# Four PSUM banks as one pool for turns, small products and down results

## The chip, the cores and the metric

The kernel runs on one core of one Trainium2 chip. The metric is the device time of one execution in microseconds; the kernel before takes 510.87 us, the median of three runs (510.63 to 511.22).

## What is computed

Eight sequences of 512 tokens of 128 features pass through three blocks: a mixture of experts with half weight, a linear attention with rotary positions, a short convolution and an output gate, and the same mixture of experts once more.

```python
x = L0_attn_hidden_states                       # (8, 512, 128), fp32
x = x + 0.5 * _L0_ffn_ref(_layernorm(x), ...)   # "layer 1"
x = x + _L0_attn_ref(_layernorm(x), ...)        # "layer 2"
x = x + 0.5 * _L0_ffn_ref(_layernorm(x), ...)   # "layer 3", same weights as layer 1

# _L0_ffn_ref: one shared expert, and the best 2 of 8 routed experts, each 128 -> 256 -> 128
shared = (silu(x @ shared_gate.T) * (x @ shared_up.T)) @ shared_down.T
probs = sigmoid(x @ router_w.T + routing_bias)
scores, indices = top_k(probs, 2); scores = scores / sum(scores)
g, u = silu(x @ gate_w[e]), x @ up_w[e]
out = shared + sum over the two chosen e of score_e * ((g * u) @ down_w[e])

# _L0_attn_ref: q, k, v, gate projections; 8 heads of 16
num = q @ (k.T @ v) * scale + sum(v);  den = q @ sum(k) * scale + seq_len
out = ((num / den + depthwise_conv5(v)) * (x @ Wg.T)) @ Wo.T
```

## The kernel before, in words

The work is cut by batch b (0 to 7; 512 tokens are 4 tiles of 128) and by layer (1, 2, 3). Batches form groups (`GROUPS`: three in layer 1, four in layer 3), and a group is routed as a whole. Its tokens are sorted by expert into rows in DRAM, 128 to a block: GpSimd scatters normalized tokens (L1151), SyncE loads blocks two at a time as a *pair* r (92 pairs, `xb`), and results go back by a store (L736) and by GpSimd's gathers (L1172). VectorE adds them to X (L1238).

A pair passes through these steps, each with an engine and a line:

- `pair_turn` (TensorE, L822): transposes of `xb` into the PSUM bank `xt_ps`; `pair_hi` (ScalarE, L1014) and `pair_lo` (VectorE, L1201) read it, as an fp32 number is multiplied as a high and a low part.
- `front` (TensorE, L839 to L841): gate and up product of one block, three matmuls of 512 columns. A unit has two halves, one bank each; its first is named j = 1. Two such units of two banks, `gu0` and `gu1`, are taken in turn. Shared experts (units S) and attention projections (units A) pass through them too (L799 to L801).
- `silu` (ScalarE, L1025) and `hid` (VectorE, L1215; L1219 for the shared expert), which makes `hs`.
- `hidden_turn` (TensorE, L872): transposes of `hs` into the bank `ht_ps`; `hT_copy` (ScalarE, L1031) copies it.
- `down` (TensorE, L881): the down product, into the first bank of the pair's own gate/up unit; `y_copy` (ScalarE, L1006) copies it out and so frees the bank. `store` follows.

PSUM has eight banks of 128 x 512 fp32: four for `gu`, one each for `ht_ps` (hidden turns, and shared down products, L892, read by L1228) and `xt_ps`, and two, `misc0` and `misc1`, for all small products: turns of normalized tokens (L908), logits (L922, L924), counts (L937), and in attention k-v products, denominators, their spreading, numerators and the output projection (L947 to L981). VectorE gives back most of them: L1271, L1284, L1367, L1456, L1461, L1471, L1486. Before the change a logits result of one group can be read into `L` only when the group before has its probabilities.

The order on each engine is written out by a planner (class `Plan`). It knows each operation's length in units of 10 ns (a front half is 73, a copy of 512 columns 50), and draws 600 random sets of shifts of the ranks; for each it schedules greedily, on the engine that is free first the ready operation of least rank among those that can start within `NEAR` = 10 units, and keeps the shortest plan. Engines then run in order, held by semaphores. `take` makes TensorE wait for the last reader of a bank before it writes there. GpSimd's scatters and gathers are spaced 160 units by the plan, except those of the first group.

```python
PACE, HOP, NEAR = 160, 16, 10
...
def take(bank, done, value):
    if bank in held:
        once.wait_ge(*held[bank])
    held[bank] = (done, value)
```

Of the kernel before, what the change touches and what calls it, by code (L numbers as in the profile page):

```python
# [6 lines left out]
P = 128  # L7
# [9 lines left out]
T = S // P  # L17
# [18 lines left out]
XT, XB, HB, YB, GB, YG, ROOMS = 6, 5, 4, 3, 3, 3, 2  # L36
# [37 lines left out]
class Plan:  # L74
# [96 lines left out]
    def route(self, i, l, g):  # L171
# [40 lines left out]
    def routed(self, r, l, g, n):  # L212
# [9 lines left out]
        op(("pair_turn", r), "PE", 25, ("load", r), back("pair_lo", 1), ("squares",))  # L222
# [5 lines left out]
        op(("hidden_turn", r), "PE", 45, ("hid", u), back("hidden_turn", 1))  # L228
# [5 lines left out]
    def attention(self, b):  # L234
# [37 lines left out]
    HELD = {"turn": "lo", "logits": "bias", "count": "based", "kv": "mask", "den": "invert", "spread": "rden_bc", "num": "attend", "project": "attended"}  # L272
# [77 lines left out]
    def schedule(self, rank):  # L350
# [4 lines left out]
        self.misc, self.xt_of, self.yg_of = {}, {}, {}  # L355
        bank = [None, None]
        ht = [None]
# [38 lines left out]
        def dynamic(key):  # L396
# [24 lines left out]
            if name in ("hidden_turn", "sdown"):  # L421
                return after(ht[0]) if ht[0] else 0
# [14 lines left out]
        def settle(key, t):  # L437
# [7 lines left out]
            if name == "hidden_turn":  # L445
                ht[0] = ("hT_copy", key[1])
            if name == "sdown":
                ht[0] = ("add", key[1], key[2], "shared")
                self.shared_order.append(key[1:3])
            if name in self.HELD:  # L450
                i = min((i for i in range(2) if not bank[i] or after(bank[i]) is not None),
                        key=lambda i: after(bank[i]) if bank[i] else 0)
                self.misc[key], bank[i] = i, (self.HELD[name], *key[1:])
            if name == "hi":
                i = min((i for i in range(XT) if not xt[i] or after(xt[i]) is not None),
# [63 lines left out]
def build(nc, x, wq, wqp, wk, wv, wg, wo, lepe_w, lepe_b, sgate, sup, sdown, gate_w, up_w, down_w,  # L519
# [8 lines left out]
    with ExitStack() as ctx:  # L528
# [10 lines left out]
        ht_ps = ps("ht_ps")  # L539
        xt_ps = ps("xt_ps")  # L540
        m0, m1 = ps("misc0"), ps("misc1")
# [40 lines left out]
        L, neg, pos = [sb(name, [P, TMAX, E]) for name in ("L", "neg", "pos")]  # L582
# [122 lines left out]
        def misc(*key):  # L705
            return (m0, m1)[plan.misc[key]]
# [80 lines left out]
        def _(pe):  # L787
# [30 lines left out]
            def pair_turn(r):  # L818
                once.wait_ge(xb_loaded[r % XB], 16 * (r // XB + 1))
                wait(once, xbt_lo_done, r)  # L820
                for j in range(width(*plan.pair[r])):
                    mm = pe.transpose(xt_ps[:, j * P:(j + 1) * P], xb[r % XB][:, j], ident)  # L822
# [44 lines left out]
            def hidden_turn(r):  # L867
                n = nth_hidden["R", r]
                once.wait_ge(h_done, n + 1)
                take("ht", hT_done, r + 1)  # L870
                for q in range(HALVES * width(*plan.pair[r])):
                    mm = pe.transpose(ht_ps[:, q * P:(q + 1) * P], hs[n % HB][:, q * P:(q + 1) * P], ident)  # L872
# [13 lines left out]
            def shared_down(l, b):  # L886
                once.wait_ge(h_done, nth_hidden["S", l, b, 1] + 1)
                take("ht", updated[b], update(l, b, "shared"))
                for t in range(T):
                    for half in range(HALVES):  # L890
                        m = nth_hidden["S", l, b, half]
                        mm = pe.matmul(ht_ps[:, t * D:(t + 1) * D], hs[m % HB][:, t * P:(t + 1) * P],  # L892
# [3 lines left out]
            def multiply_ones(n):  # L896

                for _ in range(n):
                    pe.matmul(xt_ps[:].rearrange("p (t n) -> p t n", t=T), ones_bf[:],
                              ones_bf[:].rearrange("p (o n) -> p o n", o=1).to_broadcast([P, T, P]), start=True, stop=True)  # L900

            def xn_turn(l, b):
# [4 lines left out]
                for t in range(T):  # L907
                    mm = pe.transpose((m0, m1)[m][:, t * P:(t + 1) * P], xn[:, b, t], ident)  # L908
                mm.then_inc(xnT_ready[l], 1)
                if (l, b) == (1, 0):  # L910
                    multiply_ones(WARM // 2)

            def logits(l, b):
# [4 lines left out]
                dst = (m0, m1)[m]  # L918
# [8 lines left out]
            def count(l, g):  # L927
# [5 lines left out]
                dst, n, c = (m0, m1)[m], tiles(l, g), chosen[l, g]  # L933
# [7 lines left out]
            def kv(b):  # L941
# [4 lines left out]
                for t in range(T):  # L946
                    mm = pe.matmul((m0, m1)[m][:, 0:VW], k_rot[:, t, :], v_tok[:, t, :], start=t == 0, stop=t == T - 1)  # L947
                mm.then_inc(kv_ready, 1)

            def denominators(b):  # L950
# [4 lines left out]
                for t in range(T):  # L955
                    mm = pe.matmul((m0, m1)[m][:, t * NH:(t + 1) * NH], q_rot[:, t * P:(t + 1) * P], ks_bd[:],
# [3 lines left out]
            def spread(b):  # L960
# [4 lines left out]
                for t in range(T):  # L965
                    mm = pe.transpose((m0, m1)[m][:, t * P:(t + 1) * P], wide[:, t * P:(t + 1) * P], ident)
                mm.then_inc(rbc_ready, 1)

            def numerators(b):
# [4 lines left out]
                pe.matmul((m0, m1)[m][:], kv_bd[:], q_rot, start=True, stop=True).then_inc(num_ready, 1)  # L974

            def out_project(b):
# [3 lines left out]
                for t in range(T):  # L980
                    mm = pe.matmul((m0, m1)[m][:, t * D:(t + 1) * D], oT[:, t * P:(t + 1) * P], wo_sb[:],  # L981
# [4 lines left out]
            multiply_ones(WARM)  # L986
# [6 lines left out]
        def _(act):  # L993
# [8 lines left out]
            def y_copy(r):  # L1002
# [3 lines left out]
                nc.scalar.activation(ys[r % YB][:].rearrange("p j d -> p (j d)")[:, 0:n], bank(("R", r))[:, 0, 0:n],  # L1006
                                     ACT.Copy).then_inc(y_copied, 1)

            def pair_hi(r):
# [4 lines left out]
                nc.scalar.activation(xbt_hi[r % 2][:, 0:n], xt_ps[:, 0:n], ACT.Copy).then_inc(xbt_hi_done, 1)  # L1014
# [12 lines left out]
            def hT_copy(r):  # L1027
# [3 lines left out]
                nc.scalar.activation(hT[r % 2][:, 0:n], ht_ps[:, 0:n], ACT.Copy).then_inc(hT_done, 1)  # L1031
# [155 lines left out]
        def _(dve):  # L1187
# [8 lines left out]
            def pair_lo(r):  # L1196
# [4 lines left out]
                v.tensor_tensor(xbt_lo[r % 2][:, 0:n], xt_ps[:, 0:n], xbt_hi[r % 2][:, 0:n].bitcast(F32),  # L1201
# [359 lines left out]
```

## Time and profile before

| what | value |
|---|---|
| median of three timed runs | 510.87 us |
| profiled execution, span | 540.9 us, 30.0 us above that median |
| TensorE matmul busy | 474.9 us (88%) |
| TensorE weight load busy | 381.7 us (71%) |
| VectorE busy | 348.5 us (64%) |
| ScalarE busy | 272.3 us (50%) |
| GpSimd busy | 282.4 us (52%) |

The profile is of one execution, on the only core. A busy share is the part of the span in which the engine ran an instruction; the table by stretch gives the same for parts of the span. "Idle before" is the time an engine stood before an instruction, and the releaser is whose semaphore ended it; "issue" is standing for which the profile has no reason. Matmul ends are modelled, so TensorE's busy time covers some of its standing. Timelines give start and length in microseconds.

### The profile page before, as it was taken

The page shows a single profiled execution, that of the slowest core. Times are in us where ns is not written, and L with a number is a line of the kernel's source. Part 1 is how long each engine was busy: PE and PEld are TensorE (multiplying, and loading weights), DVE is VectorE, ACT ScalarE, POOL GpSimd, SP SyncE. Part 2 cuts the span into 40 slices and gives each one's busy share as a digit, 9 for nine tenths or more (in the row PEclk, how much of TensorE's full clock was granted, in tenths as well). Part 3 has the DMA queues.
Part 4 walks back from the last instruction along what each step waited for, and adds up shares of the span by engine and source line. Part 5 has one row for each costly group of instructions (what it writes and reads, how often), then busy time and mean ns, then how long its engine had stood idle before and what let it go on. Part 6 is the DMA issues. An engine that isn't in the chain of part 4 may idle for free.

```text
span 540.9 us, 9674 instructions
## 1 busy us (share of the span) xinstructions
PE 474.9 (88%) x2975; PEld 381.7 (71%) x2975; DVE 348.5 (64%) x1064; ACT 272.3 (50%) x612; POOL 282.4 (52%) x290
## 2 busy tenths in 40 slices
PE   7894687998999999999999999999999998899980
PEld 3673676776777787777877777877777776667760
DVE  4992795322358765889996789998966224344442
ACT  5861232555566466647647556653554543443530
POOL 4167054545566506666715666776555545553543
PEclk9999799999999999999999999999999999999997
DMA  8961112234431223321132321113442433442222
GB/s 240 377 215 55 54 64 68 79 112 130 121 89 55 87 80 109 103 65 58 57 102 75 86 66 59 45 45 93 121 133 82 127 95 92 124 127 59 79 73 68
DMA packets 74352, 53.66 MB, mean 99 GB/s; under 512 B 9664, under 2 KB 68928, under 8 KB 74304
## 3 DMA queue, kind: packets, MB, share of 16 engines
q1 hardware_dynamic: 66112, 36.26, 22.4%
q0 software_dynamic: 8192, 16.79, 10.0%
q8 instruction: 26, 0.43, 0.3%
q14 instruction: 22, 0.18, 0.1%
HBM read 26.87 MB, written 26.15 MB: 98 GB/s over the span
## 4 chain that ended last, share of the span: by engine, by line
PE 53%; DVE 23%; issue 8%; ACT 7%; another core or an unknown queue 4%; DMA 2%; POOL 1%; SPq 1%; DVEq 0%; POOLq 0%; ACTq 0%
PE gu L881 15%; PE ht_ps L872 7%; PE gu L839 6%; PE gu L841 6%; PE gu L840 5%; PE xt_ps L822 3%; DVE hs L1219 2%; DVE hs L1215 2%; ACT gs L1025 2%; PE gu L799 2%; DVE raw L1415 2%; PE gu L801 1%; PE gu L800 1%; ACT xn L1048 1%
## 5 line engine op out<-in xcount | busy, mean ns | idle before, releaser
L1172 POOL DMA_INDIRECT yg<-y_sorted,places x128 | 123.0, 961 | 113.2 <-PE gu L841 72.4
L1151 POOL DMA_INDIRECT x_sorted<-xn,places x128 | 129.9, 1015 | 97.3 <-PE gu L841 36.2
L881 PEld LDWEIGHTS gu<-w,hT 128*128 128x128 f32 x708 | 87.1, 191 | 36.0 <-issue 33.7
L881 PE MATMUL gu<-w,hT 128*128 x708 | 100.3, 284 | 11.3 <-ACT hT L1031 6.7
L1025 ACT ACTIVATE gs<-gu 128x512 f32<-128x512 f32 x124 | 72.2, 583 | 53.5 <-PE gu L801 19.4
L1215 DVE TENSOR_TENSOR hs<-gs,gu 128x512 f32<-128x512 f32 x92 | 60.7, 662 | 49.6 <-ACT gs L1025 27.0
L839 PE MATMUL gu<-w,xbt_hi 128*128 x177 | 83.6, 473 | 7.1 <-ACT ys L1006 2.9
L1031 ACT ACTIVATE hT<-ht_ps 128x512 f32<-128x512 f32 x92 | 53.3, 580 | 56.6 <-PE ht_ps L872 38.8
L1201 DVE TENSOR_TENSOR xbt_lo<-xt_ps,xbt_hi 128x256 fp32r<-128x256 f32 x92 | 37.7, 410 | 64.9 <-ACT xbt_hi L1014 56.5
L841 PE MATMUL gu<-w,xbt_hi 128*128 x177 | 70.7, 399 | 0.0
L840 PE MATMUL gu<-w,xbt_lo 128*128 x177 | 70.2, 397 | 0.0
L1006 ACT ACTIVATE ys<-gu 128x256 f32<-128x256 f32 x92 | 34.4, 375 | 54.3 <-PE gu L881 41.0
L872 PE MATMUL ht_ps<-squares_sb,hs 128*128 128x128 f32 x354 | 55.5, 278 | 4.6 <-DVE hs L1215 3.5
L872 PEld LDWEIGHTS ht_ps<-squares_sb,hs 128*128 128x128 f32 x354 | 40.9, 141 | 18.7 <-DVE hs L1215 10.7
L1014 ACT ACTIVATE xbt_hi<-xt_ps 128x256 fp32r<-128x256 f32 x92 | 34.4, 373 | 27.8 <-PE gu L841 14.4
L1130 POOL TENSOR_TENSOR rstd<-ve,minus_half 128x4 f32<-128x4 f32 x24 | 26.8, 1116 | 40.0 <-DVE ve L1259 38.4
L1048 ACT ACTIVATE xn<-X,shifts,rstd 128x128 f32<-128x128 f32 x96 | 40.8, 486 | 13.3 <-DVE shifts L1263 10.1
L839 PEld LDWEIGHTS gu<-w,xbt_hi 128*128 128x128 f32 x177 | 33.8, 191 | 15.3 <-issue 13.1
L1238 DVE SCALAR_TENSOR_TENSOR X<-yg,wsel,X 128x128 f32<-128x128 f32 x128 | 36.4, 346 | 7.0 <-DMA yg<-y_sorted,places 6.5
L1219 DVE TENSOR_TENSOR hs<-gs,gu 128x512 f32<-128x512 f32 x32 | 21.8, 682 | 28.1 <-ACT gs L1025 25.7
L841 PEld LDWEIGHTS gu<-w,xbt_hi 128*128 128x128 f32 x177 | 33.6, 190 | 7.8
L822 PE MATMUL xt_ps<-squares_sb,xb 128*128 128x128 f32 x177 | 35.1, 277 | 4.2 <-DVE xbt_lo L1201 2.9
(132 smaller groups left out, 799.4 us busy)
## 6 DMA issues: line engine op xcount, KB each, us to landing
xb<-x_sorted SPq DMA_DIRECT2D x85, 128.0 KB
y_sorted<-ys SPq DMA_DIRECT2D x85, 128.0 KB
x_sorted<-yg SPq DMA_DIRECT2D x6, 512.0 KB, 5.7
X<-x_dram SPq DMA_DIRECT2D x8, 256.0 KB, 4.8
x_sorted<-xn,places POOLq DMA_INDIRECT x128
yg<-y_sorted,places POOLq DMA_INDIRECT x128
out_dram<-X SPq DMA_DIRECT2D x8, 256.0 KB
raw<-gate_w_dram SPq DMA_DIRECT2D x4, 256.0 KB, 4.3
```

What stands on the lines that cost most here:

```text
L822: mm = pe.transpose(xt_ps[:, j * P:(j + 1) * P], xb[r % XB][:, j], ident)
L839: pe.matmul(dst[:, j], xbt_hi[r % 2][:, at], hi, start=True, stop=False)
L840: pe.matmul(dst[:, j], xbt_lo[r % 2][:, at], hi, start=False, stop=False)
L841: mm = pe.matmul(dst[:, j], xbt_hi[r % 2][:, at], lo, start=False, stop=True)
L872: mm = pe.transpose(ht_ps[:, q * P:(q + 1) * P], hs[n % HB][:, q * P:(q + 1) * P], ident)
L881: mm = pe.matmul(dst[:, j * D:(j + 1) * D], hT[r % 2][:, at:at + P], w_flat[:, bass.ds(expert[r][j] + 2 * GU + half * D, D)], start=half = ...
L1025: nc.scalar.activation(dst, src, ACT.Silu).then_inc(silu_done, 1)
L1031: nc.scalar.activation(hT[r % 2][:, 0:n], ht_ps[:, 0:n], ACT.Copy).then_inc(hT_done, 1)
L1048: ins = nc.scalar.activation(xn[:, b, t], X[:, b, t], ACT.Identity, bias=shifts[:, l, b, t:t + 1], scale=rstd[:, l, b, t:t + 1])
L1151: nc.gpsimd.indirect_dma_start(x_sorted[l, g], bass.IndirectOffsetOnAxis(places[l, g][:, k, t:t + 1], 0), xn[:, b, t % T], None).then_inc( ...
L1172: nc.gpsimd.indirect_dma_start(yg[slot][:, k, t], None, y_sorted[l, g], bass.IndirectOffsetOnAxis(places[l, g][:, k, at:at + 1], 0)).then_ ...
L1215: v.tensor_tensor(hs[n % HB][:].rearrange("p (j i) -> p j i", j=2)[:, 0:k], gs[n % GB][:].rearrange("p (j i) -> p j i", j=2)[:, 0:k], bank ...
```

## The change

The banks `ht_ps`, `xt_ps`, `misc0` and `misc1` become one list of four, `pool_ps`. The planner gives a bank of it to each pair turn, hidden turn, down result and shared down result as to the small products: the free one whose last reader ends first. `down` writes to the pool, so a gate/up bank of a routed pair is freed by `hid` and not by `y_copy`. So that no result holds a bank for long without its reader being able to run, needs are added to the plan: `pair_turn` on the front of two pairs earlier (and no longer on the last `pair_lo`), `hidden_turn` on the `down` of two pairs earlier, and in attention kv, den, spread and num on steps of the batch before or on `vT`; a `turn` waits until there is room for its copy. The routing operand `L` gets a second buffer, so that logits need only the probabilities of two groups earlier. All instructions of arithmetic and transfer are the same as before; their order is planned anew.

```diff
-XT, XB, HB, YB, GB, YG, ROOMS = 6, 5, 4, 3, 3, 3, 2
+XT, XB, HB, YB, GB, YG, ROOMS, POOL = 6, 5, 4, 3, 3, 3, 2, 4
...
-        if before:
+        if i >= 2:
...
-                self.ops["bias", l, b] = (e, length, needs + [("probs", *before)], lands)
+                self.ops["bias", l, b] = (e, length, needs + [("probs", *GROUP_LIST[i - 2])], lands)
...
-        op(("pair_turn", r), "PE", 25, ("load", r), back("pair_lo", 1), ("squares",))
+        op(("pair_turn", r), "PE", 25, ("load", r), ("squares",), ("front", ("R", r - 2), 0) if r >= 2 else None)
...
-        op(("hidden_turn", r), "PE", 45, ("hid", u), back("hidden_turn", 1))
+        op(("hidden_turn", r), "PE", 45, ("hid", u), back("hidden_turn", 1), back("down", 2))
...
-        op(("kv", b), "PE", 95, ("rope_add", b), ("v_tok", b))
+        op(("kv", b), "PE", 95, ("rope_add", b), ("v_tok", b), last("num"), last("den"))
...
-        op(("den", b), "PE", 81, ("mask", b), ("q_add", b))
+        op(("den", b), "PE", 81, ("mask", b), ("q_add", b), last("widen"))
...
-        op(("spread", b), "PE", 44, ("widen", b))
+        op(("spread", b), "PE", 44, ("widen", b), last("attend"))
...
-        op(("num", b), "PE", 90, ("spread", b))
+        op(("num", b), "PE", 90, ("spread", b), ("vT", b))
...
+            "pair_turn": "pair_lo", "hidden_turn": "hT_copy", "down": "y_copy", "sdown": "add"}
...
-            return ("y_copy", u[1]), ("hid", u)
+            return ("hid", u), ("hid", u)
...
-        bank = [None, None]
-        ht = [None]
+        bank = [None] * POOL
...
-            if name in ("hidden_turn", "sdown"):
-                return after(ht[0]) if ht[0] else 0
+            if name == "turn" and sum(1 for k in xt if not k or after(k) is not None) <= len(self.turned):
+                return None
...
-                i = min((i for i in range(2) if not bank[i] or after(bank[i]) is not None),
+                i = min((i for i in range(POOL) if not bank[i] or after(bank[i]) is not None),
...
-        ht_ps = ps("ht_ps")
-        xt_ps = ps("xt_ps")
-        m0, m1 = ps("misc0"), ps("misc1")
+        pool_ps = [ps(f"pool{i}") for i in range(POOL)]
...
-        L, neg, pos = [sb(name, [P, TMAX, E]) for name in ("L", "neg", "pos")]
+        L_of = [sb(f"L{i}", [P, TMAX, E]) for i in range(2)]
+        L = {lg: L_of[i % 2][:, 0:tiles(*lg)] for i, lg in enumerate(groups)}
+        neg, pos = [sb(name, [P, TMAX, E]) for name in ("neg", "pos")]
...
-                return (y_copied, u[1] + 1), (h_done, nth_hidden[u] + 1)
+                return (h_done, nth_hidden[u] + 1), (h_done, nth_hidden[u] + 1)
...
-                wait(once, xbt_lo_done, r)
+                m = plan.misc["pair_turn", r]
+                take(m, xbt_lo_done, r + 1)
...
-                take("ht", hT_done, r + 1)
+                m = plan.misc["hidden_turn", r]
+                take(m, hT_done, r + 1)
...
-                dst = bank(("R", r))[:, 0]
+                m = plan.misc["down", r]
+                take(m, y_copied, r + 1)
+                dst = pool_ps[m]
...
-                take("ht", updated[b], update(l, b, "shared"))
+                m = plan.misc["sdown", l, b]
+                take(m, updated[b], update(l, b, "shared"))
```

## Rows read from the trace of the kernel before

**Rows 1.** The page: the span, and busy time with share and instructions.
```profile
span 540.9 us, 9674 instructions
PE 474.9 (88%) x2975; PEld 381.7 (71%) x2975; DVE 348.5 (64%) x1064; ACT 272.3 (50%) x612; POOL 282.4 (52%) x290
```
**Rows 2.** Stretches: length, busy (x instructions) by engine, granted clock, DMA share, GB/s.
```profile
57.00:60.00 3.00, 2.09 (x5) 1.71 (x6) 2.66 (x9) 1.11 (x3) 0.00 (x0) 0.50 0.61 177
...
92.00:515.00 423.00, 394.79 (x2482) 318.42 (x2481) 274.24 (x792) 229.25 (x520) 232.53 (x233) 1.00 0.30 89
...
160.00:400.00 240.00, 226.34 (x1469) 187.10 (x1468) 199.39 (x596) 138.01 (x314) 139.77 (x136) 1.00 0.26 78
```
**Rows 3.** TensorE by line, 100:515 us: busy, mean ns, then idle before and releasers.
```profile
L881 PE MATMUL gu<-w,hT 128*128 x675 | 95.7, 284 | 8.1 <-ACT hT L1031 3.8 <-issue 2.3
L839 PE MATMUL gu<-w,xbt_hi 128*128 x166 | 78.3, 472 | 6.5 <-ACT ys L1006 2.9 <-issue 1.6 <-DVE hs L1219 1.6
...
L872 PE MATMUL ht_ps<-squares_sb,hs 128*128 128x128 f32 x336 | 52.7, 278 | 4.4 <-DVE hs L1215 3.5 <-issue 0.3
L822 PE MATMUL xt_ps<-squares_sb,xb 128*128 128x128 f32 x163 | 32.3, 277 | 3.4 <-DVE xbt_lo L1201 2.8
L799 PE MATMUL gu<-xt_hi,aw_hi 128*128 128x512 f32 x32 | 13.9, 434 | 0.9 <-ACT ys L1006 0.5 <-issue 0.5
...
L799 PE MATMUL gu<-xt_hi,sw_hi 128*128 128x512 f32 x26 | 12.1, 466 | 1.9 <-ACT ys L1006 1.9
```
**Rows 4.** Timeline of two pairs: start us, length us, engine, line, operation.
```profile
111.67 0.41 PE L822 MATMUL xt_ps<-squares_sb,xb 128*128 128x128 f32 x2 [0.59 <-DVE xbt_lo L1201]
...
112.98 0.48 PE L839 MATMUL gu<-w,xbt_hi 128*128 x1
...
114.00 1.15 PE L881 MATMUL gu<-w,hT 128*128 x8
...
114.58 0.69 DVE L1215 TENSOR_TENSOR hs<-gs,gu 128x512 f32<-128x512 f32 x1 [2.82 <-ACT gs L1025]
...
114.90 0.48 PE L839 MATMUL gu<-w,xbt_hi 128*128 x1
...
115.19 0.42 DVE L1201 TENSOR_TENSOR xbt_lo<-xt_ps,xbt_hi 128x256 fp32r<-128x256 f32 x1
...
115.69 0.60 PE L872 MATMUL ht_ps<-squares_sb,hs 128*128 128x128 f32 x4
...
116.15 0.48 PE L839 MATMUL gu<-w,xbt_hi 128*128 x1
...
116.32 0.60 ACT L1031 ACTIVATE hT<-ht_ps 128x512 f32<-128x512 f32 x1 [0.75 <-PE ht_ps L872]
...
117.06 1.15 PE L881 MATMUL gu<-w,hT 128*128 x8
...
118.25 0.38 ACT L1006 ACTIVATE ys<-gu 128x256 f32<-128x256 f32 x1 [0.35 <-issue]
```
**Rows 5.** Timeline where an attention unit follows a down product.
```profile
238.44 0.38 ACT L1006 ACTIVATE ys<-gu 128x256 f32<-128x256 f32 x1 [0.84 <-PE gu L881]
...
238.88 0.50 PE L799 MATMUL gu<-xt_hi,aw_hi 128*128 128x512 f32 x1 [0.47 <-issue]
```
**Rows 6.** Waits of the whole run: who <- whom, us in total, times, longest.
```profile
POOL x_sorted L1151 <- DVE places L1379: 16.3, 2, 15.0
...
ACT gs L1025 <- remote: 11.4, 1, 11.4
...
PE gu L799 <- DVE hs L1219: 9.0, 4, 6.6
...
PE ht_ps L892 <- DVE X L1228: 3.6, 3, 1.5
...
PE xt_ps L822 <- DVE xbt_lo L1201: 2.9, 6, 0.9
```
**Rows 7.** ScalarE's copies of down results, 160:400 us, by line.
```profile
L1006 ACT ACTIVATE ys<-gu 128x256 f32<-128x256 f32 (+1 forms) x41 | 15.2, 374 | 23.9 <-PE gu L881 22.6 <-issue 1.0
```
**Rows 8.** Timeline of the end: the last adds of gathered results.
```profile
535.04 2.31 DVE L1238 SCALAR_TENSOR_TENSOR X<-yg,wsel,X 128x128 f32<-128x128 f32 x8 [6.50 <-DMA yg<-y_sorted,places]
```

More of the change, by code:

```diff
@@ L270, in attention @@
         op(("attended", b), "DVE", 60, ("project", b))
-    HELD = {"turn": "lo", "logits": "bias", "count": "based", "kv": "mask", "den": "invert", "spread": "rden_bc", "num": "attend", "project": "attended"}
+    HELD = {"turn": "lo", "logits": "bias", "count": "based", "kv": "mask", "den": "invert", "spread": "rden_bc", "num": "attend", "project": "attended",
+            "pair_turn": "pair_lo", "hidden_turn": "hT_copy", "down": "y_copy", "sdown": "add"}
     BETWEEN = ("pair_turn", "hidden_turn", "down", "regs", "pair_hi", "pair_lo", "silu", "hid", "hT_copy", "y_copy",
@@ L444, in settle @@
                 count[name] += 1
-            if name == "hidden_turn":
-                ht[0] = ("hT_copy", key[1])
             if name == "sdown":
-                ht[0] = ("add", key[1], key[2], "shared")
                 self.shared_order.append(key[1:3])
             if name in self.HELD:
-                i = min((i for i in range(2) if not bank[i] or after(bank[i]) is not None),
+                i = min((i for i in range(POOL) if not bank[i] or after(bank[i]) is not None),
                         key=lambda i: after(bank[i]) if bank[i] else 0)
-                self.misc[key], bank[i] = i, (self.HELD[name], *key[1:])
+                self.misc[key], bank[i] = i, (self.HELD[name], *key[1:], *(("shared",) if name == "sdown" else ()))
+            if name == "turn":
+                self.turned.add(key[1:])
             if name == "hi":
+                self.turned.discard(key[1:])
                 i = min((i for i in range(XT) if not xt[i] or after(xt[i]) is not None),
@@ L705, in misc @@
         def misc(*key):
-            return (m0, m1)[plan.misc[key]]
+            return pool_ps[plan.misc[key]]
         def run(engine, stages):
@@ L917, in logits @@
                 take(m, logits_read[l], b + 1)
[L918 removed]
+                dst = pool_ps[m]
                 hi, lo = xt_hi[plan.xt_of[l, b]], xt_lo[plan.xt_of[l, b]]
@@ L946, in kv @@
                 for t in range(T):
-                    mm = pe.matmul((m0, m1)[m][:, 0:VW], k_rot[:, t, :], v_tok[:, t, :], start=t == 0, stop=t == T - 1)
+                    mm = pe.matmul(pool_ps[m][:, 0:VW], k_rot[:, t, :], v_tok[:, t, :], start=t == 0, stop=t == T - 1)
                 mm.then_inc(kv_ready, 1)
@@ L973, in numerators @@
                 take(m, att_done, b + 1)
-                pe.matmul((m0, m1)[m][:], kv_bd[:], q_rot, start=True, stop=True).then_inc(num_ready, 1)
+                pe.matmul(pool_ps[m][:], kv_bd[:], q_rot, start=True, stop=True).then_inc(num_ready, 1)
             def out_project(b):
@@ L980, in out_project @@
                 for t in range(T):
-                    mm = pe.matmul((m0, m1)[m][:, t * D:(t + 1) * D], oT[:, t * P:(t + 1) * P], wo_sb[:],
+                    mm = pe.matmul(pool_ps[m][:, t * D:(t + 1) * D], oT[:, t * P:(t + 1) * P], wo_sb[:],
                                    start=True, stop=True)
@@ L1005, in y_copy @@
                 n = width(*plan.pair[r]) * D
-                nc.scalar.activation(ys[r % YB][:].rearrange("p j d -> p (j d)")[:, 0:n], bank(("R", r))[:, 0, 0:n],
+                nc.scalar.activation(ys[r % YB][:].rearrange("p j d -> p (j d)")[:, 0:n], misc("down", r)[:, 0:n],
                                      ACT.Copy).then_inc(y_copied, 1)
@@ L1013, in pair_hi @@
                 n = width(*plan.pair[r]) * P
-                nc.scalar.activation(xbt_hi[r % 2][:, 0:n], xt_ps[:, 0:n], ACT.Copy).then_inc(xbt_hi_done, 1)
+                nc.scalar.activation(xbt_hi[r % 2][:, 0:n], misc("pair_turn", r)[:, 0:n], ACT.Copy).then_inc(xbt_hi_done, 1)
             def silu(u):
@@ L1030, in hT_copy @@
                 n = width(*plan.pair[r]) * I
-                nc.scalar.activation(hT[r % 2][:, 0:n], ht_ps[:, 0:n], ACT.Copy).then_inc(hT_done, 1)
+                nc.scalar.activation(hT[r % 2][:, 0:n], misc("hidden_turn", r)[:, 0:n], ACT.Copy).then_inc(hT_done, 1)
             def round_xn(l, b):
@@ L1200, in pair_lo @@
                 n = width(*plan.pair[r]) * P
-                v.tensor_tensor(xbt_lo[r % 2][:, 0:n], xt_ps[:, 0:n], xbt_hi[r % 2][:, 0:n].bitcast(F32),
+                v.tensor_tensor(xbt_lo[r % 2][:, 0:n], misc("pair_turn", r)[:, 0:n], xbt_hi[r % 2][:, 0:n].bitcast(F32),
                                 ALU.subtract).then_inc(xbt_lo_done, 1)
@@ L1274, in biased @@
             def biased(l, b):
-                t0 = (b - GROUPS[l][group_of(l, b)][0]) * T
+                g = group_of(l, b)
+                t0 = (b - GROUPS[l][g][0]) * T
                 halves = misc("logits", l, b)[:, 0:2 * T * E].rearrange("p (t r e) -> p t r e", t=T, r=2)
-                rows = L[:, t0:t0 + T]
+                rows = L[l, g][:, t0:t0 + T]
                 once.wait_ge(logits_ready[l], b + 1)
```

36 lines of the change are left out of this document (18 added, 18 removed).

## The prediction, made before the changed kernel ran

> **What bounds the kernel now.** I read the busy shares first [rows 1]: TensorE is busy for 474.9 of 540.9 us (88%), VectorE for 64%, ScalarE for 50%. Then the table by stretch [rows 2]: from 92 us, once routed pairs run, to 515 us TensorE is busy for 394.79 of 423 us, at a granted clock of 1.00. TensorE sets the pace there, and 28.2 us of holes in its row are what a looser assignment of PSUM banks can win. VectorE comes nearest from 160 to 400 us, with 199.39 of 240. The third view groups TensorE's matmuls by line for 100 to 515 us, with the idle time ahead of each group and what ended it [rows 3]. Copies of down results (L1006 reads a gate/up bank) ended 2.9 + 0.5 + 1.9 us of it ahead of fronts, the hidden copy hT (L1031) 3.8 ahead of `down`, "issue" 2.3 there too, the single bank of pair turns (L1201) 2.8, and products `hs` 3.5 + 1.6.
>
> The fourth view is the timeline of two pairs [rows 4]. The turn of hidden states at 115.69 feeds ScalarE's copy at 116.32, and `down` starts at 117.06, which is 1.37 us after its turn; one gate/up half lies between them. From `down` at 114.00 to `down` at 117.06 is 3.06 us. TensorE's own steps in it are 0.90 (114.00 to 114.90), 0.79 (to 115.69), 0.46 with the one pair turn (to 116.15), and once more 0.79: 2.94. So 0.12 us of this period is waiting, and by the same sum 0.23 in front of the `down` at 114.00 (112.98 plus a half's 0.79 is 113.77).
>
> One bank's round: the first half filled at 112.98 is silu'd, multiplied (114.58 + 0.69 = 115.27), turned, copied, and multiplied by the down weights into the same bank, and is free when the copy at 118.25 ends, 118.63. That is 5.65 us, or 2.83 per pair over two banks, just under the 3.06 of the period. It holds only as long as nothing else takes a bank: in [rows 5] an attention unit's front stood 0.47 us and began at 238.88, right behind the copy that ended at 238.82, though the view calls it "issue".
>
> **The change, part by part.** No instruction of arithmetic or DMA is added, removed or resized: reads of PSUM only name other banks, and the second `L` buffer renames an operand. So the terms are waits and order alone. The 600 random trials are drawn anew over the changed needs, so the whole order may differ; the terms price what the freed order can take away.
>
> (a) `down` leaves the gate/up bank. It is free from the end of `hs` (115.27) rather than of the y copy (118.63): its round falls from 5.65 to 2.29 us [rows 4]. What goes are the waits behind L1006, 5.3 us, and those put down to issue ahead of the same fronts, 1.6 + 0.5 [rows 3]: 7.4 us at most. What is late next is `hs`, whose 1.6 ahead of L839 stays. I take 5.5.
>
> (b) A second half can now lie between a hidden turn and its `down`. The gap in front of `down` is 3.8 + 2.3 = 6.1 us in all [rows 3]. But the planner still takes `down`, of rank 0, if it is planned ready within its 0.1 us window (`NEAR`), and the plan's copy of 0.50 us measures 0.60 [rows 4]: such gaps stay when the order stays. Bounds 0 and 6.1; I take 2.5, nearer the lower end for that reason.
>
> (c) Pair turns and hidden turns rotate over four banks. L822 behind L1201 waits 2.8 us [rows 3], and shared down products behind the add that shares their bank 3.6 us over the run [rows 6]. The second is mostly near the start, where weights and routing run late as well, so I count 1 of it and 2 of the first: 3. The new need of `pair_turn` on the front of two pairs earlier costs nothing in TensorE order, since that front is issued earlier anyway; it removes a hold, for xt_ps is now filled at 111.67 and read last at 115.19 [rows 4].
>
> (d) `L` twice, so that logits of a group no longer hold a bank until the group before is routed. Places are waited for by GpSimd for 15.0 us once [rows 6], but in that same time ScalarE stood for 11.4 us on nothing the profile names, and VectorE's routing stood behind it. Bounds: 0, and 15.0 for a chain that TensorE never followed, since it had shared units to do. I take 0.
>
> (e) What is added: `take` on a common bank makes a pair turn, hidden turn or `down` wait for whatever reader had the bank, also a VectorE one. Queued behind it on TensorE is everything, and behind a late turn ScalarE's and VectorE's next copy. No such wait exists in the trace; the nearest row is L822 behind L1201, 2.9 us in 6 times over the run, 0.48 each [rows 6]. Demand [rows 4]: a pair holds banks for 1.5 to 3.9 us (its turn; some 1.5 for a matmul, two reads and the hand-overs, 3.9 is today's 111.67 to 115.61), 1.23 us (115.69 to 116.92) and 1.57 us (117.06 to 118.63): 4.3 to 6.7 us in 3.06, so 1.4 to 2.2 of four banks. In attention stretches half as many pairs run (41 in 240 us [rows 7]) and eight batches' six results take the rest. Four banks are enough on average. Bounds: 0, and 0.48 for each of those 41, 19.7 us. I take 1.5, from the mean demand. `hidden_turn` behind `down` of two pairs earlier is in the present order already (0).
>
> Sum: -5.5 - 2.5 - 3 + 1.5 = -9.5 us. 540.9 - 9.5 = 531.4 for the profiled span. The profiled execution is 30.0 us longer than the median of the timed runs (540.9 to 510.87), so it holds time that those lack, which no row here explains; the waits on banks follow from the order and lengths of instructions, and I carry them over unscaled: 510.87 - 9.5 = 501.4 us. The tail from 515 us isn't touched: last store, gathers, adds and output hang on one another, and the last adds stood 6.50 us for their gathers [rows 8].
>
> **Rivals.**
> Much faster: all 28.2 us of holes but the 3.5 + 1.6 behind `hs` go, since the drawn order gets room everywhere: -23 us, 488. For it: the modelled ends of matmuls hide a part of each hole, so there is more than the row shows. Against it: every saved wait lets TensorE run into the next late item.
>
> No change: the gate/up round was already 2.83 us per pair against 3.06, TensorE's own 2.94 us is the bound, and the planner orders much as before: within 1 us of 510.9.
>
> Slower: late VectorE readers. Between 160 and 400 us VectorE is busy for 199.39 of 240 us [rows 2], an in-order queue in which bias, mask, invert, attend and attended now give back the banks that pair turns take. At 0.48 us each, a wait ahead of 20 of the 41 turns eats the 9.5 us. If it stands ahead of hidden turns and `down`s as well, 35 of the 123 cost 16.8 us, which less 9.5 makes 518. That happens if holds, planned without VectorE's lateness, double from about two banks to four.
>
> Slower by the clock: were the shorter rounds to break TensorE's work into bursts, it could be granted the lower level again. In the trace it is at 0.50 (1.2 GHz) from 57 to 60 us, after TensorE's stand of 6.6 us [rows 2, 6]. Half the clock costs work at most its own time again, so 14 us of such stretches less the 9.5 give 515. But two banks rotate today in every unit, with holes all along, and the clock is 1.00 from 92 to 515 us [rows 2]. The Trainium skill, page "TensorE: Matmul & The Clock Gate", section "A second HAM failure mode: psum-queue depth-cycling", tells of a kernel that cycles through PSUM banks and whose micro-idle times make the clock swing between its levels; by that rule more rotation is a risk, while this trace disagrees, with 1.00 throughout.
>
> The stand near 45 us is a risk of both signs: ScalarE waited 11.4 us and TensorE 6.6 [rows 6] while group 0 was scattered; a new order may meet it elsewhere or miss it. I add some us to both ends for it.
>
> **From cases to numbers.** Forecast, 495 to 508 us: 0.52. Much faster, under 495: 0.12. No change, 508 to 513: 0.15. Late VectorE readers or a worse drawn order, over 513: 0.18. Clock: 0.03. The time is that of the likeliest, 501.4. For 8 in 10 the range takes in most of each case: 489 (nearly the whole of the holes) to 516. A measurement of this kernel can tell 0.2%, 1.0 us, from no change. Faster than 509.8: 0.52 + 0.12 + 0.04 of the third case = 0.68; within 509.8 to 511.9: 0.08; slower: 0.24.
>
> **What would show it.** (a) right: waits of L839 and L799 behind L1006 are gone, and L1006 isn't among those TensorE waits for. (b) right: two halves stand between a hidden turn and its `down`, and the wait behind L1031 falls under 3 us. (c) right: no L822 behind L1201. (e) wrong in my sum: new waits of L822, L872 or L881 behind L1461, L1471 or L1486. TensorE's busy time per instruction should be unchanged and its holes between 92 and 505 us be some 18 us rather than 28. The prediction is wrong if the drawn order gives up in the start or the tail what the middle wins, or if the holes stay under other names.

## The result and the profile after

| kernel | median, us | ratio to before, 95% interval |
|---|---|---|
| before | 510.75 | |
| after | 494.02 | 0.9677 (0.9663 to 0.969) |

The change takes 16.7 us off. The forecast was 501.4 us, 9.5 less, with a range of 489 to 516: the sign and the range held, and the gain was sized at 57% of what it is.

The profiled execution of the kernel before, 540.9 us, was a disturbed one that no timed run resembles; a second profile of the same kernel, taken with the experiments, spans 508.9 us, and every comparison below is made against that one. First its page and the long stretch, then those of after (stretches: length, busy by engine, granted clock, DMA share, GB/s).

```profile
span 508.9 us, 9674 instructions
PE 468.5 (92%) x2975; PEld 379.1 (74%) x2975; DVE 347.9 (68%) x1064; ACT 274.4 (54%) x612; POOL 283.1 (56%) x290
...
92.00:480.00 388.00, 371.47 (x2366) 302.33 (x2366) 267.77 (x780) 220.12 (x497) 221.87 (x222) 1.00 0.32 92
```

```profile
span 492.1 us, 9735 instructions
PE 461.1 (94%) x2975; PEld 379.6 (77%) x2975; DVE 347.3 (71%) x1064; ACT 273.0 (55%) x612; POOL 284.8 (58%) x290
...
PEclk9999999999999999999999999999999999999997
...
92.00:463.00 371.00, 360.75 (x2332) 298.68 (x2331) 263.55 (x769) 216.23 (x489) 219.25 (x218) 1.00 0.33 96
```

The same 2975 matmuls run, and the granted clock of these stretches is 1.00 in both. TensorE's visible holes in the long stretch fall from 16.5 us (388 - 371.47) to 10.3 (371 - 360.75). Its busy time falls by 7.4 us too (468.5 to 461.1). I put this down to the modelled ends, which covered some standing in before. The waits of TensorE in after, over the whole run (who <- whom: us in total, times, longest):

```profile
PE pool L897 <- DVE hs L1224: 4.4, 4, 2.1
PE pool L874 <- DVE hs L1220: 3.2, 9, 0.7
...
PE pool L885 <- ACT hT L1036: 1.5, 4, 0.5
...
PE pool L823 <- ACT ys L1011: 1.2, 2, 0.6
...
PE pool L874 <- DVE xbt_lo L1206: 0.6, 1, 0.6
PE gu L840 <- DVE hs L1224: 0.5, 1, 0.5
```

No front waits for a y copy any more, where [rows 3] had 5.3 us of it and the second profile 0.9 (L799, below); and no pair turn waits for L1206, which is L1201 of before [rows 3, 6]. The new kind of wait is there: a pair turn behind a y copy and a hidden turn behind `pair_lo`, readers of a common bank, 1.2 + 0.6 = 1.8 us.

As the profile's idle time hides what matmul ends cover, I also took the distance from each matmul's start to the next, and counted what it exceeds the lower quartile of the same pair of kinds by, all runs below together. The excess is put down to the matmul that came late. This is worked out from the traces' start times, in us:

| kernel | pair turns | fronts | shared down | down | hidden turns | all | first to last matmul | span |
|---|---|---|---|---|---|---|---|---|
| before, second profile | 12.8 | 12.6 | 6.9 | 19.1 | 13.6 | 89.2 | 494.6 | 508.9 |
| old order, pool, down in gate/up | 7.6 | 15.4 | 3.3 | 19.0 | 13.9 | 85.6 | 491.5 | 506.5 |
| old order, all new banks | 8.7 | 11.2 | 3.3 | 20.7 | 12.9 | 83.0 | 488.6 | 503.6 |
| after | 6.0 | 4.5 | 6.3 | 20.6 | 12.4 | 74.6 | 480.5 | 492.1 |
| after, copy planned at 0.60 | 5.1 | 6.9 | 6.1 | 14.1 | 12.2 | 77.9 | 483.4 | 488.0 |

(Fronts here are the first matmuls of halves.) The levels in this table depend on how finely the kinds are drawn: with each line, step and shape as a kind of its own, "all" is 65.7, 62.4, 59.6, 51.9 and 52.7 us from top to bottom. The changes among the first three rows, and that of "all" from before to after, come out within 1 us of the table's. The fall of pair turns from the old order to after doesn't hold (2.9 and 3.0 us with the finer kinds). The column from first to last matmul needs no kinds.

From before to after the matmul stream is 14.1 us shorter, of which 14.6 is excess, and what lies around it 2.7 us: 14.3 to 11.6.

### The profile page after: what moved, and what is told of

The parts are those of the page before. It is cut to its first block, busy times and chain, and to the rows that moved or that the text cites. A ratio compares the mean times of both kernels' runs of the same rounds, so it can differ in the third digit from the quotient of the medians.

```text
span 492.1 us, 9735 instructions
## 1 busy us (share of the span) xinstructions
PE 461.1 (94%) x2975; PEld 379.6 (77%) x2975; DVE 347.3 (71%) x1064; ACT 273.0 (55%) x612; POOL 284.8 (58%) x290
## 4 chain that ended last, share of the span: by engine, by line
PE 31%; DVE 13%; issue 3%; ACT 2%; POOL 1%; DMA 1%; POOLq 0%; DVEq 0%
PE pool L885 8%; PE pool L874 4%; PE gu L840 4%; PE gu L842 3%; PE gu L841 3%; DVE X L1243 2%; DVE raw L1421 2%; PE pool L823 1%; DVE hs L1220 1%; POOL yg L1177 1%; PE pool L897 1%; PE gu L799 1%; ACT gs L1030 1%; PE gu L801 1%; PE gu L800 1%
## 5 line engine op out<-in xcount | busy, mean ns | idle before, releaser
L885 PEld LDWEIGHTS pool<-w,hT 128*128 128x128 f32 x708 | 87.0, 191 | 27.0 <-issue 24.8
L885 PE MATMUL pool<-w,hT 128*128 x708 | 99.3, 284 | 3.6 <-ACT hT L1036 1.5
L1011 ACT ACTIVATE ys<-pool 128x256 f32<-128x256 f32 x92 | 34.6, 376 | 62.2 <-PE pool L885 59.1
L1036 ACT ACTIVATE hT<-pool 128x512 f32<-128x512 f32 x92 | 53.1, 579 | 24.9 <-PE pool L874 23.8
L874 PE MATMUL pool<-squares_sb,hs 128*128 128x128 f32 x354 | 54.6, 276 | 4.0 <-DVE hs L1220 3.2
L874 PEld LDWEIGHTS pool<-squares_sb,hs 128*128 128x128 f32 x354 | 40.7, 141 | 16.4 <-DVE hs L1220 12.2
L1053 ACT ACTIVATE xn<-X,shifts,rstd 128x128 f32<-128x128 f32 x96 | 40.9, 487 | 11.6 <-DVE shifts L1268 11.6
L1206 DVE TENSOR_TENSOR xbt_lo<-pool,xbt_hi 128x256 fp32r<-128x256 f32 x92 | 37.3, 409 | 14.0 <-ACT xbt_hi L1019 13.4
L1019 ACT ACTIVATE xbt_hi<-pool 128x256 fp32r<-128x256 f32 x92 | 34.0, 373 | 5.1 <-PE pool L823 5.0
L897 PE MATMUL pool<-swd,hs 128*128 128x128 f32 x256 | 31.7, 277 | 4.4 <-DVE hs L1224 4.4
L823 PE MATMUL pool<-squares_sb,xb 128*128 128x128 f32 x177 | 34.0, 273 | 1.8 <-ACT ys L1011 1.2
```

Of the source, the lines that this page charges most:

```text
L874: mm = pe.transpose(pool_ps[m][:, q * P:(q + 1) * P], hs[n % HB][:, q * P:(q + 1) * P], ident)
L885: mm = pe.matmul(dst[:, j * D:(j + 1) * D], hT[r % 2][:, at:at + P], w_flat[:, bass.ds(expert[r][j] + 2 * GU + half * D, D)], start=half = ...
L1036: nc.scalar.activation(hT[r % 2][:, 0:n], misc("hidden_turn", r)[:, 0:n], ACT.Copy).then_inc(hT_done, 1)
L1053: ins = nc.scalar.activation(xn[:, b, t], X[:, b, t], ACT.Identity, bias=shifts[:, l, b, t:t + 1], scale=rstd[:, l, b, t:t + 1])
```

## The experiments

### The kernel before, profiled again

No edit.

> The kernel before once more, for a second profile. The first profiled execution lasted 540.9 us where timed runs take 510.75; of the changed kernel they are 492.1 and 494.0. If the 30 us were a disturbance of that one execution, this span comes to some 509, the stands near 45 and 88 us are gone, and the holes of TensorE between 92 us and its last routed pairs are fewer than 28 us. If they belong to the kernel under the profiler, the span is near 540 again.

Measured: 510.73 us, span 508.9. The disturbance belonged to the one execution. Without it the wait of ScalarE for 11.4 us [rows 6] is gone, and the rows that carried my terms shrink:

```profile
L881 PE MATMUL gu<-w,hT 128*128 x708 | 100.2, 285 | 4.3 <-ACT hT L1031 1.0 <-issue 0.8
L839 PE MATMUL gu<-w,xbt_hi 128*128 x177 | 83.1, 470 | 3.3 <-DVE hs L1219 2.2 <-issue 0.4 <-DVE hs L1215 0.2
...
L822 PE MATMUL xt_ps<-squares_sb,xb 128*128 128x128 f32 x177 | 35.1, 277 | 3.0 <-DVE xbt_lo L1201 1.7 <-issue 0.6
L892 PE MATMUL ht_ps<-swd,hs 128*128 128x128 f32 x256 | 31.9, 278 | 4.9 <-DVE X L1228 4.0 <-DVE hs L1219 0.8
...
L799 PE MATMUL gu<-xt_hi,aw_hi 128*128 128x512 f32 x32 | 13.9, 435 | 0.9 <-ACT ys L1006 0.9
```

(By line: busy, mean ns, then idle before and its releasers.) Ahead of L839 not one wait is put down to the y copy, where [rows 3] had 2.9 us, ahead of L799 0.9 instead of 0.5 + 1.9, and ahead of L881 the copy hT accounts for 1.0 instead of 3.8. Only the shared down products behind L1228, 4.0 us, are what they were.

### The old order with the new banks

The order of all five engines is taken, operation for operation, from the plan of the kernel before; the banks are given and freed as after the change. The needs added to the plan are left out, since the old order doesn't always keep them.

```diff
+        self.forced = {e: list(keys) for e, keys in OldPlan().order.items()}
...
             for key in waiting:
+                e = ops[key][0]
+                if self.forced[e][len(self.order[e])] != key:
+                    continue
```

> The new banks with the order of the kernel before, operation for operation on all five engines: only the waits differ. My sum priced just this: waits that go (-5.5 - 2.5 - 3, of which the 2.5 ahead of down needs another order) and +1.5 for new ones, so -7 us, 504. Rival, the order is the gain: within 1.5 us of the kernel before. Rival, waits are all of the gain: 494 to 496.

Measured: 505.03 us, ratio 0.9881 (0.9865 to 0.9898), -5.7 us by the medians. Looser waits alone are a third of the gain, and close to the 7 that my sum held for them; the other 11.0 us, to 494.0, come with the new order.

```profile
L1257 PE MATMUL pool<-squares_sb,xb 128*128 128x128 f32 x177 | 34.6, 274 | 1.4 <-issue 0.6 <-ACT ys L1445 0.5 <-DMA xb<-x_sorted 0.2
L1331 PE MATMUL pool<-swd,hs 128*128 128x128 f32 x256 | 31.7, 278 | 1.7 <-DVE hs L1658 1.7
```

L1257 is the pair turn (L822) and L1331 the shared down product (L892) of this file: the waits behind `pair_lo` and behind L1228 are gone, 3.0 to 1.4 and 4.9 to 1.7 us of idle time.

### The old order with the pool, down results left where they were

As above, but `down` writes into its gate/up bank, which the y copy frees.

```diff
-            "pair_turn": "pair_lo", "hidden_turn": "hT_copy", "down": "y_copy", "sdown": "add"}
+            "pair_turn": "pair_lo", "hidden_turn": "hT_copy", "sdown": "add"}
...
-                dst = pool_ps[m]
+                dst = bank(("R", r))[:, 0]
```

> The order of the kernel before, operation for operation, with the pool of four banks for turns, small products and shared down results, but down results in the gate/up banks and these freed by the y copy as before. The profile of the old order with all new banks (505.0) says that most of its 5.7 us came ahead of pair turns and shared down products (term c), little ahead of fronts (term a). If so: 505 to 507 here too. If the freed gate/up bank carries it: 509 to 511.

Measured: 508.28 us, ratio 0.9947 (0.9934 to 0.9961), -2.7 us by the ratio. It lies between the two expectations. At a fixed order, then, the pool (term c, less what sharing its banks costs) gives 2.7 us (2.0 to 3.4 by the interval), and taking down results out of the gate/up banks (term a) another 3 (508.28 to 505.03; by the ratios 3.4, uncertain by about 1 us). The table agrees: from before to here pair turns and shared down products lose 8.8 us of excess while fronts gain 2.8, now the next late item; from here to all new banks fronts lose 4.2.

### Each part alone, with an order of its own

Down results alone: they share the two banks of small products, everything else as before.

```diff
-    HELD = {..., "num": "attend", "project": "attended"}
+    HELD = {..., "num": "attend", "project": "attended", "down": "y_copy"}
...
-            return ("y_copy", u[1]), ("hid", u)
+            return ("hid", u), ("hid", u)
...
-                dst = bank(("R", r))[:, 0]
+                m = plan.misc["down", r]
+                take(m, y_copied, r + 1)
+                dst = (m0, m1)[m]
```

> Only down results leave the gate/up banks, and share the two banks of small products; turns keep one bank each, L is single. The order is planned anew. If the gate/up round is the part that matters: most of the gain, 496 to 501. If the pool is what matters, because two banks are too few for small products and down results: 505 to 512.

The pool alone: the changed kernel with down results back in the gate/up banks.

> The other part alone: four banks as a pool for turns, small products and shared down results, two L buffers and the new needs, but down results stay in the gate/up banks, which wait for their copies as before. If the gate/up round is the part that matters: 507 to 513, no better than before. If the pool matters: 498 to 503.

Measured: 512.46 us for down results alone, ratio 1.0028 (1.0007 to 1.0049), and 510.94 for the pool alone, ratio 1.0005 (0.9993 to 1.0017). At this draw neither half gains anything by itself. For down results alone the trace shows where the time goes, in the stretch where two banks have to serve down results and attention's six small products a batch:

```profile
280.00:320.00 40.00, 32.02 (x191) 26.32 (x190) 36.85 (x120) 17.51 (x39) 27.56 (x26) 0.87 0.13 38
320.00:330.00 10.00, 9.51 (x41) 8.43 (x42) 8.05 (x23) 3.86 (x8) 4.62 (x4) 0.67 0.29 87
```

```profile
PE misc L925 <- DVE xt_lo L1274: 2.3, 3, 1.3
...
PE misc L959 <- DVE ks_bd L1460: 1.6, 2, 1.1
PE misc L937 <- DVE chosen L1343: 1.3, 1, 1.3
PE misc L950 <- DVE place_f L1370: 1.1, 1, 1.1
```

From 280 to 320 us TensorE works 32.02 of 40 us, and its waits are for VectorE's small steps of attention and routing, one behind the other. Of these four rows (the waits of the whole run) only the last is for a bank (k-v products, L950, behind the reader of a count, L1370); the others wait for their operands. By the trace's down products 44 of the 92 pairs are done at 300 us and 46 at 350, where the kernel before has done 53 and 56: no down product ends between 252.5 and 339.5 us. The plan itself is so, with none between 244.9 and 327.4 us. That the two banks forced the planner to this is likely and not shown. The granted clock adds to it: in this profile TensorE is busy for 24.6 us at 1.2 GHz, which costs up to half of that (last section).

The first time lies 0.5 us above its second case and the second in its first, so each run puts the gain on the other's part. The planner's own lengths, read from the four plans, are 501.8 us for before, 493.0 for after, 500.3 for down results alone and 509.4 for the pool alone. So the pool alone was given an order that already the planner holds for 7.6 us worse than before's. With seeds 2 and 3 the plan is 501.3 and 489.9 us for down results alone, 503.9 and 510.6 for the pool alone; none of these ran. A draw of the order weighs as much as what is to be measured, as the next runs show.

### Other draws of the order

Only the seed of the planner's 600 trials is changed, in both kernels.

```diff
-ROUNDS, SEED = 600, 1
+ROUNDS, SEED = 600, 2
```

> The kernel before with another draw of the planner's 600 trials (SEED = 2), nothing else. If draws matter little: within 2 us of 510.8. If the first draw was a lucky one, by which the change was measured too low: 513 to 518.

> The kernel before with SEED = 3. As for SEED = 2: within 2 us of 510.8, or 513 to 518 if the first draw was lucky.

> The changed kernel with SEED = 2. If what it won comes from its banks and not from its draw, it lies within 3 us of 494.0. If the gain over the old order (505.0 to 494.0) was the luck of one draw: 500 to 507.

> The changed kernel with SEED = 3, the draw whose plan the planner itself holds for longer than the first by some 11 us. If the plan's length carries over to the chip: 503 to 507. If it doesn't: 494 to 499.

| seed | before, us | after, us | difference |
|---|---|---|---|
| 1 | 510.8 | 494.0 | -16.7 |
| 2 | 517.0 | 501.0 | -16.0 |
| 3 | 521.0 | 510.3 | -10.8 |

Each expectation had a case for a lucky first draw. The kernel before falls into it with seed 2 and beyond it with seed 3; the changed kernel falls into it with seed 2 (501.0) and with seed 3 lies 3 us over what its longer plan had given. The first draw was lucky, then, for both. Draws move either kernel by up to 10 and 16 us, as much as the change itself. But at each of three seeds the new banks win, by 14.5 us on average. So the gain isn't the luck of one draw of the new kernel; how it divides into waits and order is measured for the first only. That the new order is one which the old banks forbid can be read from the plans: held to the order of after, the planner of before comes to a stop ahead of the 27th of TensorE's operations, a turn of normalized tokens. The plans' lengths are 501.8, 508.1 and 510.4 us before and 493.0, 493.2 and 504.2 after. They foresee gains of 8.8, 14.9 and 6.1 us, so at seed 1 about half of the gain isn't in the plan.

A part of the spread is the clock. The profile of after with seed 3 has TensorE busy at 1.2 GHz for 13.7 us, that with seed 2 for 6.8, and before has none with seeds 2 and 3 and in its second profile. At half the speed this is up to 6.8 and 3.4 us of their times. The ten runs with seed 3 go from 509.2 to 515.7 us, and the four over 514 are those with the lowest mean clock (0.968 to 0.975, the others 0.979 to 0.983). So a comparison of single draws, such as that of the two halves at seed 1, is uncertain by some 10 us, and that neither half can be called worthless; only "not worth the whole" is shown for them.

The same for a fourth seed of the changed kernel, whose plan the planner holds for the shortest:

> The changed kernel with SEED = 5, the draw of eleven that the planner holds for the shortest, 5.9 us under the first one. If the plan's length carries over: 487 to 491. If the first draw was lucky on the chip beyond its plan, as seeds 2 and 3 suggest (501.0 and 510.3 for plans of 0.2 and 11.2 us more): 494 to 499.

Measured: 491.18 us, ratio 0.9619 (0.9591 to 0.9648). Of the 5.9 us that this plan is shorter by, 2.8 arrived on the chip; it lies just outside the first expectation and under the second. Seeds 1 and 2 have plans within 0.2 us and are 7 us apart on the chip, of which the clock is up to 3.4: the plan's length ranks orders roughly, no more.

### The length of one copy in the plan

```diff
-        op(("hT_copy", r), "ACT", 50, ("hidden_turn", r), back("down", 2))
+        op(("hT_copy", r), "ACT", 60, ("hidden_turn", r), back("down", 2))
```

> The changed kernel, with one length of the plan set to what the trace shows: the copy of the turned hidden states 0.60 us instead of 0.50. By the plan's order 6 instead of 35 of the 92 down products then have under 0.95 us of TensorE work between their turn and them. If term (b) failed because the plan still puts down where it thinks the copy done: the waits ahead of down fall by several us, and the time to 487 to 492 if the new draw gives nothing back. If those waits are what TensorE needs anyway to change over to the down product: they stay, and the time is 494 give or take the draw, up to 504.

Measured: 489.95 us, ratio 0.9601 (0.9569 to 0.9633), the fastest of all. The weight loads of the down product, in the kernel before, in after, and here (busy, mean ns, idle before):

```profile
L881 PEld LDWEIGHTS gu<-w,hT 128*128 128x128 f32 x708 | 87.1, 191 | 28.1 <-issue 25.6
```

```profile
L885 PEld LDWEIGHTS pool<-w,hT 128*128 128x128 f32 x708 | 87.0, 191 | 27.0 <-issue 24.8
```

```profile
L885 PEld LDWEIGHTS pool<-w,hT 128*128 128x128 f32 x708 | 87.1, 191 | 14.3 <-issue 10.0
```

The change left this wait where it was, 28.1 and 27.0 us, and one corrected length halves it. In the timeline of after the old figure is still there:

```profile
110.81 1.15 PE L885 MATMUL pool<-w,hT 128*128 x8
...
112.50 0.60 PE L874 MATMUL pool<-squares_sb,hs 128*128 128x128 f32 x4
...
113.14 0.60 ACT L1036 ACTIVATE hT<-pool 128x512 f32<-128x512 f32 x1 [0.76 <-PE pool L874]
...
113.88 1.15 PE L885 MATMUL pool<-w,hT 128*128 x8
...
116.65 1.15 PE L885 MATMUL pool<-w,hT 128*128 x8
```

From hidden turn to `down` it is 1.38 us with one half between, and from `down` to `down` 3.07, as in [rows 4] (1.37 and 3.06); the next period is 2.77. By the plans one half lies between in 79 of the 92 pairs before, in 70 after and in 60 here, and two or more in 4, 11 and 18. Yet the 4.1 us that this kernel gains can't be booked to the wait. The table has 6.5 us less ahead of down (20.6 to 14.1) but more ahead of attention products, and 3.3 more in all (0.8 with the finer kinds). The largest of what came in for it is a wait of the k-v products, 0.2 us in after:

```profile
L952 PE MATMUL pool<-v_tok,k_rot 128*128 128x130 f32 x64 | 8.8, 279 | 4.2 <-DVE k_rot L1445 4.2
```

Its stream of matmuls is 2.9 us longer; what it saves is behind it, as 4.6 us instead of 11.6 lie around the stream. By the start times 109 matmuls come after its last down product, 53 in after and 38 before: independent shared products run while GpSimd gathers the last results. So the forecast about the wait held, and what it is worth stays open, as the draw changed with it.

### A pool of three banks

```diff
-YG, ROOMS, POOL = 6, 5, 4, 3, 3, 3, 2, 4
+YG, ROOMS, POOL = 6, 5, 4, 3, 3, 3, 2, 3
```

> The changed kernel with a pool of three banks instead of four, one PSUM bank left unused; the order is planned anew. My sum held the pool for half used (1.4 to 2.2 of four banks by pairs). If so: the waits on readers of a bank (L823, L874, L885 behind y copies, pair_lo, small products) rise from 1.8 us to at most 5 and the time is 494 to 500. If four banks are just enough: such waits of over 8 us, and over 503.

Measured: 499.02 us, ratio 0.9762 (0.9742 to 0.9781). Five microseconds over after, and 12 under the kernel before with one bank of PSUM fewer.

```profile
PE pool L874 <- DVE hs L1220: 7.0, 14, 1.8
PE pool L939 <- DVE L L1290: 5.3, 1, 5.3
```

One wait is for a bank without doubt: a count stood 5.3 us until VectorE had read logits (L1290). With 0.3 us each behind L1477 and, twice, L1206, 0.2 behind it once more and 0.5 behind L1373, readers of banks make some 6.9 us, between the 5 and the 8 of the expectations; the time is on the side of a pool with room. The clock fell during that one stand: from 40 to 50 us it is 0.71 and from 50 to 60 0.78, and TensorE is busy at 1.2 GHz for 8.0 us, up to 4.0 us of cost. The stand and its clock together are more than the 5.0 us between the two kernels. As far as one draw tells, four banks have room and three begin to pinch, at a long-held result and not on average.

## Why the prediction was right, and where its sum was off

**What bounds the kernel** held: TensorE, 92% busy before and 94% after, and the gain is standing taken from it. The two profiles have the same matmuls by line. One sign that I gave failed: TensorE's busy time per instruction was to stay, and it fell by 7.4 us in all. And the holes went from 16.5 to 10.3 us rather than from 28 to 18, since some 12 of the 28 belonged to the disturbed execution.

**(a) Down out of the gate/up bank**, -5.5 in the sum: 3 us at a fixed order. It was sized from waits of the disturbed profile, 5.3 us behind L1006. The second profile shows 0.9 us of these ahead of matmuls, so neither profile's rows give the 3. At the fixed order 4.2 us of excess ahead of fronts go, and 1.7 come in ahead of down.

**(b) A second half ahead of down**, -2.5: nothing. The reason that I gave for taking little, the planner's short copy, seems to account for half of the wait: idle time of the weight loads is 28.1 and 27.0 us before and after, and 14.3 with the copy's length mended. One half still lies between hidden turn and `down` in 70 of 92 pairs, where the sign for (b) asked for two. The other sign, under 3 us behind L1031, is met with 1.5 us and tells nothing, as the second profile of before has 1.0. I should have taken the bound, 0.

**(c) Turns that rotate**, -3: 2.7 measured at a fixed order, net of what sharing the banks costs. Right in size. I had counted 2 for pair turns and 1 for L1228; by idle time with all new banks it is the other way (1.6 and 3.2 us less), by excess it is as I had it (5.2 and 3.6 us less with the pool), so the split stays open.

**(d) Two L buffers**, 0: not run by itself. With the old need and one buffer put back, the planner gives the same order on every engine and the same bank to each result, so that run would have repeated the changed kernel in all but an operand's address. This is read from the plans, not from a chip.

**(e) Waits on common banks**, +1.5: 1.8 us in the trace of after, of which 0.6 is behind a VectorE reader (`pair_lo`). The readers that the slower rival names (bias, mask, invert, attend, attended) hold TensorE up only where banks are short, most of all L1290 with three banks, 5.3 us.

**The step that failed** is the sentence under which I priced "what the freed order can take away" by the waits of the present order. The old order with new banks, 505.0, is what that sum describes, and its -7 to the 5.7 measured is near, in part by luck: (a) was taken 2 us too large, and (c) with (e) too small. The other 11.0 us come with an order that the old banks don't allow: [rows 3] can only show an order's own waits, not those that a planner avoids by giving up a better order. I had put this into the "much faster" rival with 0.12. The second miss is "the tail isn't touched": the 20.1 us from the last down product to the end became 21.7, but 53 instead of 38 matmuls run in them, and what lies around the matmul stream is 2.7 us shorter.

**The rivals.** No change and the slower ones didn't come about at this draw. The rival by the clock didn't either: after has a granted clock of 1.00 from 92 to 463 us with four banks rotating. But other draws of the same kernel did lose clock, so its chance of 0.03 was low and its cause another one (last section). I had also read the clock of before as 1.00 throughout from 92 us on. The 1.00 of [rows 2] is a mean over 423 us: from 92 to 97 us it was 0.66, after a stand of 2.9 us. That the measured time fell where it did is partly luck of the draw: with SEED = 3 the changed kernel measured 510.3, inside "no change" against the 510.75 of before, while before itself took 521.0 with that seed. I had the draw only as "a worse drawn order", in a case with another rival, and its spread unmeasured.

## What to carry to other kernels

When a planner or a search writes the order, waits seen in the trace price only the present order; hold the order fixed once with the new resources to learn what the waits are worth, and draw both sides at several seeds before believing a gain or a loss under the spread (here 10 to 16 us). Look at the granted clock of each variant before comparing times. Compare lengths in the plan with lengths in the trace: one copy 0.10 us too short kept half of the wait ahead of down alive through a change meant to loosen it. And take a second profile where the first one's span lies far from the timed median.

## What the hardware showed that I had not expected

The granted clock fell in stretches in which TensorE was mostly busy. With down results in two banks it is 0.87 from 280 to 320 us and 0.67 from 320 to 330, so part of them ran at 1.2 GHz, with six stands of 0.9 to 1.4 us between 283 and 320 us. It isn't only a matter of too few banks. The changed kernel with SEED = 3 rotates through its four banks and has

```profile
370.00:380.00 10.00, 7.92 (x45) 6.78 (x44) 6.97 (x23) 4.96 (x11) 0.00 (x0) 0.86 0.30 84
380.00:390.00 10.00, 10.00 (x60) 8.87 (x60) 7.53 (x34) 4.85 (x12) 1.03 (x1) 0.80 0.14 40
```

after a hidden turn stood 1.7 us for `hs` at 376 us. With SEED = 5 it is 0.83 from 280 to 290 us, where a hidden turn stood 2.8 us for `hs`. At the lower clock shared down products start 0.213 us apart in all five traces that have some there, and 0.112 at the full one, so work takes about twice as long. From this comes my estimate of the cost, half of TensorE's busy time at 1.2 GHz between the start and the last matmul: up to 12.3 us with down results alone (24.6 busy), 6.8 for seed 3 (13.7), 4.0 for three banks (8.0), 3.4 for seed 2 (6.8), 3.1 for seed 5 (6.3), and none for after, the copy planned at 0.60, the pool alone, the two old orders, the second profile of before and before with seeds 2 and 3. A stand by itself doesn't decide it: after stood 1.9 us at 8.6 us and kept its clock.

The Trainium skill, page "TensorE: Matmul & The Clock Gate", section "A second HAM failure mode: psum-queue depth-cycling", describes micro-idle times between groups of matmuls, in a kernel that cycles through PSUM banks, as a way in which the clock comes to swing. These traces agree that the clock falls after idle times in a busy stretch. They don't show that the cycling brings it: after rotates through four banks at 1.00 from 92 to 463 us, and the stands ahead of the falls with seeds 3 and 5 were for `hs`, a result of VectorE, and with three banks for a bank held long.

In the one disturbed execution ScalarE stood for 11.4 us, VectorE for 10.5 and TensorE for 6.6, ending at 56.5 to 57.9 us, while group 0 was being scattered [rows 6]. The second profile has the same scatters and no such stand, and I don't know its cause.
